# Two-layer tower on one core: the first layer's expert products change from fp32 operands to fp16 high and low parts

## The reference

```python
H = jax.nn.gelu(xf @ W1 + b1, approximate=False)            # 64 -> 256
probs = jax.nn.softmax((H @ Wg + bg) / TEMP, axis=-1)       # 8 experts
assign = jnp.argmax(probs, axis=-1)
out = jnp.zeros_like(xf)
for e in range(Wd.shape[0]):
    y = H @ Wd[e] + bd[e]                                   # 256 -> 64
    sel = (assign == e)[:, None]
    out = out + jnp.where(sel, probs[:, e:e + 1] * y, 0.0)
```

## Time and profile before

| | us |
|---|---|
| median of 3 runs | 4979.21 (4976.12 to 4985.41) |
| span of the profiled execution | 4982.3 |
| PE busy in the span | 4651.3 (93%) |
| DVE | 3648.7 (73%) |
| ACT | 3173.7 (64%) |
| POOL | 2208.7 (44%) |

### The profile page before, as it was taken

One profiled execution on the slowest core, in us unless ns is written; L12 is line 12 of the kernel. 1 busy time (PEld: TensorE's weight loads), 2 busy tenths in 40 slices (PEclk: granted clock), 3 DMA queues, 4 the chain that ended last, 5 costly groups with the idle time before them and its releaser, 6 DMA issues. The chain is left out here.

```text
span 4982.3 us, 122822 instructions
## 1 busy us (share of the span) xinstructions
PE 4651.3 (93%) x42323; PEld 2070.5 (42%) x42323; DVE 3648.7 (73%) x6356; ACT 3173.7 (64%) x3464; POOL 2208.7 (44%) x2149
## 2 busy tenths in 40 slices
PE   5999979999999999999999979999999999999965
PEld 3444423333333333333333334444444444444433
DVE  4666656666666666666666678888888888888878
ACT  2443426666666666666666648888888888888844
POOL 2233243333332323233333346566666666666656
PEclk9999989999999999999999979999999999999966
DMA  4211100000000000000000000000000000000001
GB/s 101 68 51 51 51 1 2 1 2 1 2 1 2 1 2 1 2 1 2 1 2 1 1 1 3 3 3 3 3 3 3 3 3 3 3 3 3 3 7 27
DMA packets 43766, 52.86 MB, mean 11 GB/s; under 512 B 33416, under 2 KB 33544, under 8 KB 43144
## 3 DMA queue, kind: packets, MB, share of 16 engines
q1 hardware_dynamic: 40440, 44.03, 3.4%
q10 hardware_dynamic: 2704, 0.72, 0.1%
HBM read 39.73 MB, written 4.19 MB: 9 GB/s over the span
## 5 line engine op out<-in xcount | busy, mean ns | idle before, releaser
L1686 DVE TENSOR_REDUCE a_mp<-psum 128x1 f32<-128x512 f32 x2072 | 1325.2, 686 | 674.3 <-PE psum L1563 669.9
L2412 DVE TENSOR_REDUCE f_mp<-psum 128x1 f32<-128x512 f32 (+2 forms) x2352 | 1475.3, 684 | 212.8 <-PE psum L2234 200.0
L1531 ACT ACTIVATE a_prob<-psum,escale 128x1024 f32<-128x1024 f32 x1024 | 1087.0, 1110 | 534.3 <-PE psum L1612 533.9
L2194 ACT ACTIVATE f_prob<-psum,escale_f 128x1024 f32<-128x1024 f32 x1152 | 1247.4, 1112 | 226.2 <-PE psum L2303 109.9
L1620 PE MATMUL psum<-a_prob,a_v 128*64 128x512 f32 x4104 | 993.9, 605 | 0.0
L2048 POOL TENSOR_SCALAR f_hi<-f_raw,part 128x512 f16<-128x512 f32 x324 | 506.5, 1563 | 418.1 <-ACT f_raw L2152 411.8
L2234 PE MATMUL psum<-f_kf,f_qf 64*128 64x512 f16 (+2 forms) x3658 | 657.7, 309 | 35.5 <-DVE f_mp L2412 24.8
L1451 POOL TENSOR_TENSOR a_u<-a_og,a_inv 128x512 f32<-128x512 f32 x129 | 134.4, 1042 | 1166.1 <-DVE a_inv L1701 1166.1
L2324 PE MATMUL psum<-f_prob,f_vh 128*32 128x512 f32 (+3 forms) x6144 | 614.7, 495 | 6.3 <-DVE f_oc L2434 5.6
L2303 PE MATMUL psum<-f_qf,f_kf 64*128 64x512 f16 (+3 forms) x3074 | 505.6, 329 | 39.9 <-ACT f_og L2157 18.2
L1620 PEld LDWEIGHTS psum<-a_prob,a_v 128*64 128x64 f32 x4104 | 248.9, 136 | 504.9 <-issue 498.7
(11 more groups left out here) (440 smaller groups left out, 6749.0 us busy)
## 6 DMA issues: line engine op xcount, KB each, us to landing
idx<-in_itok_BS_dram SPq DMA_DIRECT2D x36, 512.0 KB, 6.3
idx<-in_itok_BS_dram SPq DMA_DIRECT2D x54, 256.0 KB, 7.6
idx<-in_x_dram SPq DMA_DIRECT2D x18, 256.0 KB, 3.7
a_qh<-a_rowT SPq DMA_DIRECT2D x258, 1.0 KB
out_dram<-h SPq DMA_DIRECT2D x16, 256.0 KB, 2.6
f_qf<-f_rowT SPq DMA_DIRECT2D x130, 4.0 KB, 1.7
wd<-in_L_ffn_Wd_dram SPq DMA_DIRECT2D x2, 256.0 KB
bd<-in_L_ffn_bd_dram ACTq DMA_DIRECT2D x16, 2.0 KB
```

Of the source, the lines that this page charges most:

```text
L1531: act.activation(prob[:, part], k.psum[:, pair:pair + 2].rearrange("p b n -> p (b n)"), ACT.Exp, scale=k.escale[:]).then_inc(s.read, 1)
L1686: dve.tensor_reduce(mp[:, tg % 2, t + 4 * r, c:c + 1], bank_of(j + r), X, ALU.max)\
L2194: act.activation(prob[:, u % NPF], k.psum[:, pair:pair + 2], ACT.Exp, scale=k.escale_f[:])\
L2412: dve.tensor_reduce(side[:, at[0]:at[-1] + 1:step], bank_of(j + r)[:, 0:len(at) * width].rearrange("p (a b) -> p a b", b=width), X, ALU.ma ...
```

## The change

The expert product is computed from fp16 parts instead of fp32 operands. For a matrix A, `hi = fp16(A)` and `lo = fp16(A - hi)`. A tile is then three products for each of the two chunks, added up in PSUM: lo x hi, hi x lo, hi x hi.

- The weights' parts `wdhi` and `wdlo` (128 x 1024 each) are made once, on GpSimd, at the end of `setup`; `wd` itself becomes a temporary of `setup`.
- The activations' parts are made for four tiles (512 tokens, both chunks: 128 x 1024) at a time, in a pair of buffers. For chunk u = 0 to 3 of a pair ScalarE copies `hT` to `hhi` (`high`), and GpSimd subtracts (`low`). `L_HIGH` puts `high` 0 and 1 at the end of slot 1, 2 in slot 5 and 3 in slot 7. GpSimd makes `low` 0 and 1 ahead of its first sums, `low` 2 behind the sums m = 1 and `low` 3 behind m = 3.
- Tiles 0, 4, 8 and 12 wait for `hlo`; `high` 2 and 3 wait until the tiles that read their buffer are done.
- To make room: `kf` is written over `lowk`, `rs` is halved, and `moments` uses `xt` instead of `hc`.

```diff
+L_HIGH = {1: (0, 1), 5: (2,), 7: (3,)}
...
+            wd = k.wd[:].rearrange("p a e c -> p a (e c)")
+            need(pool, "ones_set")
+            signal(pool.tensor_copy(k.wdhi[:], wd), "wd_hi")
+            need(pool, "wd_hi")
+            signal(pool.tensor_tensor(k.wdlo[:], wd, k.wdhi[:], ALU.subtract), "wd_lo")
...
+                def low(pair, u):
+
+                    j, at = u // 2, slice(u % 2 * HALF, (u % 2 + 1) * HALF)
+                    passed(pool, k.seen, E["hhi"], pair * 4 + u + 1)
+                    pool.tensor_tensor(hlo[:, u % 2], hT[:, j, :, at], hhi[:, u % 2], ALU.subtract).then_inc(E["hlo"], 1)
+
                 def back(pair):
 
+                    for u in range(2):
+                        low(pair, u)
                     for m in range(8):
                         sums(pair, m)
+                        if m % 2 and m < 4:
+                            low(pair, 2 + m // 2)
...
+                def high(pair, u):
+
+                    j, at = u // 2, slice(u % 2 * HALF, (u % 2 + 1) * HALF)
+                    if u < 2:
+                        done("gelu", pair * 4 + 4)
+                    else:
+                        done("y", pair * 16 + 4 * u - 4)
+                    act.activation(hhi[:, u % 2], hT[:, j, :, at], ACT.Copy).then_inc(E["hhi"], 1)
...
+                    if back is not None:
+                        for u in L_HIGH.get(n, ()):
+                            high(back, u)
...
+                    if n % 4 == 0:
+                        done("hlo", pair * 4 + n // 4 + 1)
                     bank = ps[6 + n % 2]
+                    side, tokens = n // 4 % 2, slice(n % 4 * P, (n % 4 + 1) * P)
                     for c in range(2):
-                        last = pe.matmul(bank, lhsT=hT[:, j, c, t * P:(t + 1) * P], rhs=k.wd[:, c].rearrange("p e c -> p (e c)"),
-                                         start=(c == 0), stop=(c == 1))
+                        pe.matmul(bank, lhsT=hlo[:, side, c, tokens], rhs=k.wdhi[:, c], start=(c == 0), stop=False)
+                        pe.matmul(bank, lhsT=hhi[:, side, c, tokens], rhs=k.wdlo[:, c], start=False, stop=False)
+                        last = pe.matmul(bank, lhsT=hhi[:, side, c, tokens], rhs=k.wdhi[:, c], start=False, stop=(c == 1))
                     last.then_inc(E["y"], 1)
...
-        kf = sb("l0_kf", [P, 2, T, C], F32)
+        kf = lowk = sb("l0_lowk", [P, 2, T, C], F32)
...
-        hc = sb("l0_hc", [P, T, C], F32)
+                    hc = xt[:, j]
```

More of the change, by code:

```diff
@@ L96, in weight_loads @@
     k.bias = k.early("bias", [P, 2, HALF], F32)
+    k.wdhi = k.early("wdhi", [P, 2, EXPERTS * C], FP16)
+    k.wdlo = k.early("wdlo", [P, 2, EXPERTS * C], FP16)
     tmp = k.tmp
@@ L137, in weight_loads @@
     k.fgn = tmp("fgn", [NH, 2, C], F32)
+    k.wd = tmp("wd", [P, 2, EXPERTS, C], F32)
     k.fg2 = tmp("fg2", [P, NH], F32)
@@ L321 @@
     pool=["clear", "consts", "max_all", "fc_twice", "spread0", "low00", "high00", "low01", "high01", "spread1", "low10", "high10", "low11", "high11", "hl_bias", "hl_rest", "mgate_ones",
-          "fmax_all", "ones_set"],
+          "fmax_all", "ones_set", "wd_hi", "wd_lo"],
 )
@@ L643 @@
             "vx", "kf", "qf", "ctx", "cx", "num", "den", "aT", "proj", "x2", "cen3", "sq3", "var3", "sd3", "xn3",
-            "hid", "gelu", "gate", "lg", "eg", "tr", "xt", "y", "y_taken", "pt", "tree", "h", "var4", "sd4", "gT", "gturn", "wsel", "wturn", "wT", "cc", "rs", "bc", "numS")
+            "hid", "gelu", "gate", "lg", "eg", "tr", "xt", "y", "y_taken", "pt", "tree", "h", "var4", "sd4", "gT", "gturn", "wsel", "wturn", "wT", "cc", "rs", "bc", "numS", "hhi", "hlo")
 class Link:
@@ L672, in layer0 @@
         sd = sb("l0_sd", [P, 2, HALF // 2], F32)
-        rs = sb("l0_rs", [P, 2, HALF], F32)
+        rs = sb("l0_rs", [P, 2, HALF // 2], F32)
         x = sb("l0_x", [P, 2, HALF], F32)
@@ L676, in layer0 @@
         lowq = sb("l0_lowq", [P, 2, HALF], F32)
-        lowk = sb("l0_lowk", [P, 2, T, C], F32)
+        kf = lowk = sb("l0_lowk", [P, 2, T, C], F32)
         qf = sb("l0_qf", [P, 2, HALF], F32)
-        kf = sb("l0_kf", [P, 2, T, C], F32)
         vx = sb("l0_vx", [P, 2, T, C + 1], F32)
@@ L686, in layer0 @@
         hT = sb("l0_hT", [P, 2, 2, S], F32)
+        hhi = sb("l0_hhi", [P, 2, 2, HALF], FP16)
+        hlo = sb("l0_hlo", [P, 2, 2, HALF], FP16)
         xt = sb("l0_xt", [P, 2, T, C], F32)
@@ L1133, in moments @@
                     link(dve.tensor_scalar(mean, mean, 1.0 / C, None, ALU.mult))
-                    link(dve.tensor_tensor(hc[:], here, wide(mean, C), ALU.subtract))
-                    link(dve.tensor_tensor(hc[:], hc[:], hc[:], ALU.mult))
-                    dve.tensor_reduce(k.rstd[:, ds(b * T, T)], hc[:], X, ALU.add).then_inc(E["var4"], 1)
+                    link(dve.tensor_tensor(hc, here, wide(mean, C), ALU.subtract))
+                    link(dve.tensor_tensor(hc, hc, hc, ALU.mult))
+                    dve.tensor_reduce(k.rstd[:, ds(b * T, T)], hc, X, ALU.add).then_inc(E["var4"], 1)
                 def slot(link, n, front, back):
```

1 line of the change is left out of this document (removed).

## The result

The changed kernel took 5021.23 us (median of 4 runs, 5019.74 to 5023.96) where the kernel before took 4982.31 beside it: ratio 1.008, 95% interval 1.0066 to 1.0095. It is 0.8% slower; forecast were 4981 us and a range up to 4994. The profiled execution took 5023.96 with a span of 5022.2, 39.9 over the span of before. Some of it is in the first layer, where the forecast looked; most is in the second layer, whose code the change does not touch.

What follows compares the result with a forecast made beforehand. TensorE was taken to bound the first layer's passes (70.7 of 74.4 us). Passes -7.3, setup +3.4 and epilogue +5.9 summed to +2.0: 4981 us, range 4958 to 4994.

Steps and rivals of the forecast that it cites:

- Other edits, all at 0: First layer: kf in lowk's place, hc in xt's, smaller rs, wd as temporary, low(2), high(2) and high(3) cost nothing.
- the sum: Whole kernel: seven passes and the clock fall already paid -7.3, setup +3.4, epilogue +5.9, together +2.0 us.
- Weight loads are not hidden: Rival, TensorE's expert tiles: a tile takes 1.94 us, +43 in all, 5022 us; chance 0.06.
- Setup: End of setup on GpSimd: cast (1.04) and subtraction (2.12) behind the memset, +3.4 us, all on the path.
- The product, the path: First layer's passes: new tile 1.29 us, saving 0.43; nine of 16 tiles on the path, 3.87 per pass.
- nine times 0.43: Saving per pass from tiles 4, 5, 6, 8 to 12 and 15; tiles 2, 3, 7, 13, 14 save 0.
- the 0.3 of the weights' turn: Ahead of tiles 0 and 1: shorter tiles let the weights' turn come earlier, a gain of 0.3 us.
- VectorE's stop: Ahead of tiles 0, 1: VectorE's two scalings wait for GpSimd's low parts, +2.15 us; residual 1.84 later per pass.
- The clock: Each first-layer pass, around the centring product: longer TensorE waits lower the granted clock, +1.16 us per pass.
- Epilogue: First layer's epilogue: low(2), low(3) between GpSimd's sums +4.24, late logits less two tiles' saving +1.7, together +5.9 us.

Runs made afterwards that it cites:

- 136 and 120: 136 TensorE instructions the change itself adds, and 120 idle ones added to the changed kernel behind its first layer: 4986.41 us, ratio 1.0006 to before.
- all three kernels: Changed kernel (5021.23 us), kernel before plus 136 idle TensorE instructions (5023.20 us), changed kernel plus 8 idle TensorE instructions (5018.27 us).

## Why the prediction was wrong

- **The failed step** is "Other edits, all at 0" and with it the sum, which ended where the first layer ends. The second layer, 4276 of the 4982 us, was put at nothing without a reason. The change's own product count was in the text (two fp32 products by six fp16 ones) but not what it does to the length of TensorE's stream. 136 more instructions moved the feed-forward loop's head to a dozen instructions before the end of a fetched block: +33.0 us in that loop, most of the 39.9 by which the span grew; 4.3 more went with the clock in the attention. The trace of before shows one stall of 2.8 to 3.3 us at each return, and could have raised the question of where the loop's head lies; it has no row for the price of a second stall. No rival held this. "Weight loads are not hidden" has 5022 us, and was wrong all the same: products are 0.216 apart.
- **Setup**: mis-sized, 3.4 for 10.9. The work was right (1.04, 2.11); the 7.05 us ahead of the subtraction were missed, though the like of them, 6.69, stood in the trace of before.
- **The product, the path**: 1.30 a tile, as taken (1.29). The undisturbed pass without any stop is 69.71, so the tiles gave 4.66 where nine times 0.43, with the 0.3 of the weights' turn, are 4.17. The 0.49 more is about one tile on the path that the forecast had beside it; which one is open.
- **VectorE's stop**: the mechanism held, and so did the rule of the Trainium skill, "SBUF — State Buffer", section "Who interferes with whom", that the prediction cites. The low parts came when forecast, 15.8 us into the pass. The size was 1.70 for 2.15: a stopped scaling ends 0.29 behind GpSimd's instruction, where I had put 0.45 and 0.4, and the two low parts end 0.3 earlier than I had added up.
- **The clock**: forecast as falling in each pass. An undisturbed 71.42 stands in three of seven. If what the passes took beyond that is put down to the falls, they cost 6.4 us in seven passes (506.3 less 7 x 71.42) and 2.8 before (523.4 less 7 x 74.37), net 3.6 where 7.0 were forecast. With the undisturbed pass (-2.95 for -2.03, 6.4 us in seven) that is all of the 9.8 by which the passes beat the forecast.
- **Epilogue**: 5.4 for 5.9, and by the path that was argued: against the epilogue's start the first eviction comes 2.4 later (2.5 forecast), and GpSimd's last sum ends 5.4 later. Most of the 2.4 is a stop not of the choosing but of the norm's square ahead of it (2.63 for 0.69).

## What to carry to other kernels

A change that lengthens an engine's stream moves every loop behind it against the borders of the instruction fetches; before a difference in untouched code is explained by anything else, add idle instructions until the stream is longer by 256 in all, as 136 and 120 were here, and compare. Then look at every loop and not only at the one to be mended: twenty idle instructions mended the feed-forward loop and stalled the attention's. On GpSimd, a step from `partition_all_reduce` to tensor_tensor cost 7 us and one back 6, so keep such steps off the end of a block. A GpSimd tensor_tensor stopped VectorE's tensor_scalar and its operations with two SBUF inputs for up to 1.9 of its 2.1 us: put it beside work with slack.

## What was not expected of the hardware

- A return of the feed-forward loop costs TensorE 2.8 to 3.9 us of idle time, and 2.1 to 3.0 more where the second stall comes 4 or 12 products and weight loads behind the head. A return of the attention loop costs 1.6 to 2.1, and 0.85 to 1.19 more where it comes 20 behind.
- The clock makes a gain in one place uncertain: with one stall at each return the low stretches at the feed-forward loop's returns came to anything from 0 to 41 us, and the loop took 1843.5 us at the one end and 1864.9 at the other, about half of the difference in low clock. With two stalls they were 54.6 in all three kernels.
